# Layer 0 attention: the causal mask of the row maxima moves from TensorE's mask matmuls into VectorE's add-and-minimum instructions

## The reference

```python
Wdkv = x @ latent_w + latent_b
q = jnp.einsum('btc,hcl->bhtl', x, Wd_w) + Wd_b[None, :, None, :]
scores = jnp.einsum('bhtl,bsl->bhts', q, Wdkv) / jnp.asarray(np.sqrt(d_head), dtype=x.dtype)
causal = jnp.tril(jnp.ones((t, t), dtype=bool))
scores = jnp.where(causal[None, None, :, :], scores, -jnp.inf)
attn = jax.nn.softmax(scores, axis=-1)
y = jnp.einsum('bhts,bsl->bhtl', attn, Wdkv)
z = jnp.transpose(y, (0, 2, 1, 3)).reshape(b, t, h * Wdkv.shape[-1])
return z @ out_w + out_b
```

## Time and profile before

| | |
|---|---|
| median of 3 runs | 1755.58 us (1755.29 to 1759.24) |
| profiled execution, first to last instruction | 1746.9 us; its time outside that is not listed, and the median is 8.7 us over the span |
| PE busy | 1511.2 us (87%) |
| DVE busy | 1119.7 us (64%) |
| ACT busy | 997.0 us (57%) |
| POOL busy | 933.4 us (53%) |
| mean granted TensorE clock | 0.956 of full speed |
| mask matmuls L1843, first to last start | 45.2 to 791.5 us |
| one step | about 22.4 us (218 instructions of L962 in 610 us, eight to a step) |

### The profile page before, as it was taken

The page is one execution under the profiler, slowest core; times in us unless marked ns, Lnnn a source line. Parts: engine busy times, 40 slices in busy tenths (PEclk is TensorE's granted clock), DMA queues, the critical chain, the costliest instruction groups (busy, mean ns, idle before and its releaser), DMA issues. The chain is left out here.

```text
span 1746.9 us, 44836 instructions
## 1 busy us (share of the span) xinstructions
PE 1511.2 (87%) x14050; PEld 1109.0 (63%) x14051; DVE 1119.7 (64%) x2639; ACT 997.0 (57%) x2526; POOL 933.4 (53%) x1639
## 2 busy tenths in 40 slices
PE   4798999999999999998999488888888888885773
PEld 4655555555555555555998377777777777764662
DVE  3365555555555555553555399999899988985661
ACT  3343555555555555554332588888888888862441
POOL 6233555555555555554443666666666666632663
PEclk9998999999999999999999699999999999995875
DMA  7412222222222221223332021121211212116444
GB/s 197 133 29 57 55 55 55 55 55 55 56 56 56 56 56 56 56 59 75 68 70 60 22 49 45 41 44 43 46 43 41 44 44 45 42 31 123 89 90 113
DMA packets 240879, 107.53 MB, mean 62 GB/s; under 512 B 145465, under 2 KB 229242, under 8 KB 240762
## 3 DMA queue, kind: packets, MB, share of 16 engines
q1 hardware_dynamic: 230586, 93.23, 22.4%
q0 software_dynamic: 10240, 13.64, 3.7%
HBM read 61.92 MB, written 40.16 MB: 58 GB/s over the span
## 5 line engine op out<-in xcount | busy, mean ns | idle before, releaser
L670 POOL TENSOR_SCALAR_AFFINE_SELECT probs<-probs 128x512 f32<-128x512 f32 x256 | 183.5, 740 | 160.0 <-ACT probs L1515 160.0
L962 DVE TENSOR_REDUCE mneg<-bankS 128x2 f32<-128x256 f32 x256 | 107.2, 419 | 221.5 <-PE bankS L1848 220.9
L1515 ACT ACTIVATE probs<-bankT 128x1024 f32<-128x1024 f32 x128 | 131.0, 1023 | 185.2 <-PE bankT L1861 185.2
L963 DVE TENSOR_REDUCE mneg<-bankS 128x2 f32<-128x512 f32 x256 | 174.3, 681 | 0.0
L1510 ACT ACTIVATE qT<-bankA,bd 128x256 f32<-128x256 f32 x256 | 107.5, 473 | 95.0 <-PE bankA L1830 95.0
L1830 PE MATMUL bankA<-xnT,wd 128*128 128x256 f32 x512 | 149.7, 416 | 0.0
L663 POOL CAST qb<-qT 128x256 bf16<-128x256 f32 x256 | 97.1, 398 | 96.5 <-ACT qT L1510 96.3
L1858 PE MATMUL bankT<-qT,kT 37*128 37x512 f32 x512 | 136.9, 611 | 7.5 <-DMA qT<-mT 5.4
L1319 DVE STREAM_TRANSPOSE pt<-pe 128x768 f32<-128x768 f32 x128 | 124.4, 972 | 25.3 <-ACT pe L1600 25.1
L1875 PE MATMUL bankB<-probs,vaug 128*64 128x512 f32 x512 | 139.0, 621 | 1.1 <-ACT yT L1522 1.0
L1522 ACT COPY yT<-bankB 128x512 f32<-128x512 f32 x128 | 75.0, 586 | 82.1 <-PE bankB L1879 82.1
(11 more groups left out here) (316 smaller groups left out, 4315.6 us busy)
## 6 DMA issues: line engine op xcount, KB each, us to landing
rzb<-reciprocals SPq DMA_DIRECT2D x128, 128.0 KB
yT<-yT SPq DMA_DIRECT2D x64, 128.0 KB
xtab<-tab SPq DMA_DIRECT2D x32, 192.0 KB, 2.0
xs_sorted<-zeros SPq DMA_DIRECT2D x1, 4608.0 KB, 18.5
qT<-xs_sorted SPq DMA_DIRECT2D x144, 32.0 KB, 1.7
ys_sorted<-qT SPq DMA_DIRECT2D x36, 128.0 KB, 1.9
value_rows<-vrow SPq DMA_DIRECT2D x32, 128.0 KB, 1.8
vx<-value_rows SPq DMA_DIRECT2D x256, 16.0 KB, 1.8
```

The costliest lines, as they stand in the source:

```text
L670: pool.affine_select(out=blocks, in_=blocks, compare_op=ALU.is_ge, fill=0.0, base=0, pattern=[[0, 4], [1, P]], channel_multiplier=-1).then ...
L962: dve.tensor_reduce(mneg[:, n.half, :, j, 0], bankS[:, :, 0:128], AX.X, ALU.max, negate=True)
L963: dve.tensor_reduce(mneg[:, n.half, :, j, 1], bankS[:, :, 128:384], AX.X, ALU.max, negate=True).then_inc(S["red_done"], 1)
L1515: act.activation(pT[:, g % 2].rearrange("p e j t -> p e (j t)"), bankT[:, 0:2, :], ACT.Exp, scale=SCALE0).then_inc(S["exp_done"], 1)
```

## The change

The four mask matmuls of each `smax` go, with the constants `rowsel` and `rowneg` and the twelve GpSimd selections that make them. A constant `causal` of 128 x 256 float32 takes their place: 128 columns of zero, then the 128 x 128 mask with -1e30 above the diagonal. `red` now adds it to the scores while it takes the maximum: `tensor_tensor_reduce` computes (scores + mask) * -1 element by element, writes that to a scratch tile `masked`, and gives the minimum of a row, which is the negated maximum. One instruction does one row range of one head, so there are four instead of two. A `passed(dve)` stands ahead of them.

```diff
-            for e in range(2):
-                r = HALVES[e]
-                pool.affine_select(out=rowsel[r, 0, :], in_=rowsel[r, 0, :], compare_op=ALU.not_equal, fill=1.0, base=0,
-                                   pattern=[[-1, P]], channel_multiplier=1)
...
+            pool.affine_select(out=causal[:, P:2 * P], in_=causal[:, P:2 * P], compare_op=ALU.is_ge, fill=NEG, base=0,
+                               pattern=[[-1, P]], channel_multiplier=1)
...
             def red(n, j):
                 dve.wait_ge(S["s_ps"], n.b * PAIRS + (j + 1))
-                dve.tensor_reduce(mneg[:, n.half, :, j, 0], bankS[:, :, 0:128], AX.X, ALU.max, negate=True)
-                dve.tensor_reduce(mneg[:, n.half, :, j, 1], bankS[:, :, 128:384], AX.X, ALU.max,
-                                  negate=True).then_inc(S["red_done"], 1)
+                passed(dve)
+                for e in range(2):
+                    dve.tensor_tensor_reduce(masked[:, e, 0:P], bankS[:, e, 0:P], causal[:, P:2 * P], -1.0, -NEG, ALU.add, ALU.min,
+                                             mneg[:, n.half, e, j, 0:1])
+                for e in range(2):
+                    ins = dve.tensor_tensor_reduce(masked[:, e, P:3 * P], bankS[:, e, P:3 * P], causal[:, :], -1.0, -NEG, ALU.add, ALU.min,
+                                                   mneg[:, n.half, e, j, 1:2])
+                ins.then_inc(S["red_done"], 1)
...
-                for k in range(2):
-                    for e in range(2):
-                        blocks = bankS[:, e, 0:384].rearrange("p (i h c) -> p i h c", h=2, c=LP)[:, 0:3:2, k]
-                        pe.matmul(blocks, rowsel[HALVES[e], k, :], rowneg[HALVES[e], k, :].unsqueeze(1).to_broadcast([LP, 2, LP]),
-                                  start=(k == 0), stop=False, skip_group_check=True)
                 for e in range(2):
-                    pe.matmul(bankS[:, e, 0:128], qb[ROWS[e], j, 0:P], kb[ROWS[e], 0:P], start=False, stop=True, skip_group_check=True)
+                    pe.matmul(bankS[:, e, 0:P], qb[ROWS[e], j, 0:P], kb[ROWS[e], 0:P], start=True, stop=True, skip_group_check=True)
```

More of the change, by code:

```diff
@@ L155, in program @@
         ys_d = nc.dram_tensor("ys_sorted", [TILES * P, C], F32).ap()
-        rowsel = sb("rowsel", [P, 2, P], BF16)
-        rowneg = sb("rowneg", [P, 2, LP], BF16)
+        causal = sb("causal", [P, 2 * P])
+        masked = sb("masked", [P, 2, 3 * P], BF16)
         wd = sb("wd", [P, PAIRS, 2, LP])
@@ L558, in _ @@
             pool.memset(identb[:, :], 0.0)
[L559 to L562, removed]
+            pool.memset(causal[:, :], 0.0).then_inc(S["cst"], 1)
             pool.wait_ge(S["cst"], 3)
@@ L567, in _ @@
                                    pattern=[[-1, P]], channel_multiplier=1)
-            for e in range(2):
-                r = HALVES[e]
-                pool.affine_select(out=rowsel[r, 0, :], in_=rowsel[r, 0, :], compare_op=ALU.not_equal, fill=1.0, base=0,
-                                   pattern=[[-1, P]], channel_multiplier=1)
[L572 to L583, removed]
+            pool.affine_select(out=causal[:, P:2 * P], in_=causal[:, P:2 * P], compare_op=ALU.is_ge, fill=NEG, base=0,
+                               pattern=[[-1, P]], channel_multiplier=1)
             pool.affine_select(out=strict[:, :], in_=strict[:, :], compare_op=ALU.is_gt, fill=0.0, base=0,
                                pattern=[[1, P]], channel_multiplier=-1).then_inc(S["consts"], 1)
-            made = 7
+            made = 3
             def chain(ins):
@@ L1839, in smax @@
                     pe.wait_ge(S["red_done"], n.b * PAIRS + j)
-                for k in range(2):
-                    for e in range(2):
-                        blocks = bankS[:, e, 0:384].rearrange("p (i h c) -> p i h c", h=2, c=LP)[:, 0:3:2, k]
-                        pe.matmul(blocks, rowsel[HALVES[e], k, :], rowneg[HALVES[e], k, :].unsqueeze(1).to_broadcast([LP, 2, LP]),
-                                  start=(k == 0), stop=False, skip_group_check=True)
                 for e in range(2):
-                    pe.matmul(bankS[:, e, 0:128], qb[ROWS[e], j, 0:P], kb[ROWS[e], 0:P], start=False, stop=True, skip_group_check=True)
+                    pe.matmul(bankS[:, e, 0:P], qb[ROWS[e], j, 0:P], kb[ROWS[e], 0:P], start=True, stop=True, skip_group_check=True)
                 for e in range(2):
-                    ins = pe.matmul(bankS[:, e, 128:384], qb[ROWS[e], j, P:T], kb[ROWS[e], :], start=False, stop=True, skip_group_check=True)
+                    ins = pe.matmul(bankS[:, e, P:3 * P], qb[ROWS[e], j, P:T], kb[ROWS[e], :], start=True, stop=True, skip_group_check=True)
                 ins.then_inc(S["s_ps"], 1)
```

## The result

The changed kernel takes 1778.95 us (median of 4 runs, 1773.95 to 1782.39), the kernel before on the same chip 1756.11 (4 runs, 1755.29 to 1759.24): a ratio of 1.0124, 95% interval 1.0101 to 1.0147.

A forecast was written before the change was run, and what follows sets the result against it. Waits for VectorE's `red` were taken to hold PE in four links per step. Terms summed to +1.64 us a step, +46 for 28 steps, +3 for the first three: 1755.6 + 49 = 1805 us, range 1785 to 1845.

The forecast's parts named there:

- R: Time from first start to last end of a `red` on VectorE; forecast to grow from 1.02 to 1.47 us.
- links 0-1, 3-4, 5-6: Stretches from one `smax` to the next where PE waits for `red`; each forecast from 1.67 to 2.09 us, +0.42.
- link 1-2, with the reciprocal: From `smax` 1 to 2, also delayed by a reciprocal waiting for a DMA; forecast +0.42, less 0.2 us.
- links 2-3, 4-5: From `smax` 2 to 3 and 4 to 5, where PE's own work sets the pace; forecast to gain 0.13 us each.
- `smax` 6 to `kv` and on to the next 0: `red` 6, `normalise` and `red` 7 in a row on DVE; forecast from 4.02 to 4.44 us until `kv`, +0.42.
- The bound: In four links per step PE is held briefly by waits for `red`, hidden by its overlapping records.
- I take 0.07: Price in us of each accumulator read in `red`; four make 0.28, and the last one's tail adds 0.08.
- the cover: PE's work that hid `red` 7 ahead of `kv`, with 0.16 us to spare; forecast to be used up.
- The marker: `passed` between the wait and `red`'s first instruction; costs between 0 and 0.24 us, taken as 0.10.
- The reciprocal's delay: The reciprocal's DMA wait delays `red` 1; with a later `smax` 1 it was to go, -0.2 us a step.
- The rival in which the reads ride along: Accumulator reads in `red` add no spacing, `red` takes 1.20 us, not slower: 1756 us; chance 0.08.
- The rival of no overlap: Each `red` instruction waits until the one before leaves the engine; +5.24 us a step, 1908 us; chance 0.20.

The follow-up runs named there:

- e1: Fused masking instructions and the marker added to the kernel before, with the mask matmuls kept on PE; 1790.6 us, ratio 1.0190.
- e2: The kernel before without mask matmuls and without fused instructions, so the scores go unmasked into the old reductions; 1737.9 us, ratio 0.9889.
- e9: The kernel before with only the marker `passed(dve)` added ahead of the two old reductions; 1762.8 us, ratio 1.0041.
- e12: The changed kernel with VectorE's reciprocal moved behind the reduction of pair 1; 1764.2 us, ratio 1.0042 against the kernel before.
- e5: The kernel before with the first two `av` matmuls of a group drawn ahead of `smax` 2 and 4; 1758.5 us, ratio 1.0021.

## Why the prediction was wrong

| term of a step, us | forecast | measured |
|---|---|---|
| R | 1.02 to 1.47 | 1.02 to 1.19 |
| scores of a `smax` to the first main | 0.37 to 0.47 | 0.37 to 0.53 |
| links 0-1, 3-4, 5-6 | +0.42 each | +0.22 to 0.23 each |
| link 1-2, with the reciprocal | +0.42 - 0.2 | +0.24 |
| links 2-3, 4-5 | -0.13 each | -0.13 each |
| `smax` 6 to `kv` and on to the next 0 | +0.42 | -0.06 |
| sum | +1.64 | +0.60 |
| 28 steps | +46 | +17 |
| first three steps | +3 | +0.2 (fourth step's first scores: 174.8 to 175.0) |
| clock at half in 5 steps | not in the sum | +8 |

The last scores of layer 0 start 24.4 us later (791.6 to 816.0); the table has 25. What lies behind them, which no kernel of the study changes, takes 955 to 965 us in the 14 traces, and the fourth step's first scores lie at 170.3 to 177.3 us: so much do single executions differ, and +0.2 is no measurement of that term.

*The bound was right.* In the step shown `smax` 1, 2, 4 and 6 start 0.15 to 0.16 us behind the last read, with the waits written beside them, and e1 and e2 show it by halves. PE's falling busy time was a gain of 18 us alone (e2), which the 35 us of VectorE's half (e1) outweigh.

*The step that failed* is "I take 0.07, since a read has one element per partition and comes behind an instruction of the same kind of stream". The mains were right (0.215 and 0.34 forecast, 0.21 and 0.345 measured), and the four reads cost nothing between them; only the last one's 0.08 stands at the end. That is 0.28 us of R, in four links and twice in 6 to `kv`. The price was taken from tiny instructions back to back; those read an input, while the row of the read has no input (`mneg<-`). The prediction's own lower bound was right, but its range stopped at 1785, which no row supported; nor does a free marker give it, since 0.10 in four links and once ahead of `kv` is 0.5 us a step, 14 us, and so 1791.

*`smax` 6 to `kv`* followed from R: 0.53 from scores to `red` 6, 1.11 until `normalise` (420.71 to 421.82), 1.03 until `red` 7 (422.85), 1.18 until its last read ends (424.03), 0.14 to `kv` at 424.17, in all 3.99. The form of the sum held; with R at 1.19 the cover was not used up.

*The marker* costs 0.11 (e9), as taken. From the scores to the first main it is 0.53, though, and not 0.47: 0.05 beyond the marker was not foreseen, and no run shows where it comes from.

*The reciprocal's delay did not go.* The term of -0.2 let `smax` 1 come later and left the reciprocal's DMA where it was: "their DMAs are no later against PE than before, beyond 0.15 us". The trace shows otherwise. On SyncE that DMA (L372) stands behind the four DMAs of the maxima (L364), which wait for `red` 7. First after, then before:

```profile
424.52 2.24 SPq L364 DMA_DIRECT2D qT<-mT  x4
...
429.98 0.57 SPq L372 DMA_DIRECT2D dq<-remainders  x1
```

```profile
419.36 0.57 SPq L372 DMA_DIRECT2D dq<-remainders  x1
```

It is issued 5.95 us behind the end of `red` 7 after (424.03) and 5.96 before (413.40), and it lands about 8 us behind that end in every trace that shows its landing (medians 7.99 to 8.12). A longer `red` 7 thus comes back as a later reciprocal in the next step. `red` 7 ends 0.33 us later against the next step's scores, since `kv` had room (it stood 0.31 behind `red` 7 and now stands 0.14 behind it) and the masks ahead of the scores are gone. So the reciprocal starts 2.39 us behind the scores of `smax` 0 instead of 2.04 (medians), and the scores of `smax` 1 moved by 0.22 only. In e1 the reciprocal starts at 2.20 and `smax` 1 comes at 1.98; there link 1 to 2 is 1.99, like its equals of 1.98, and the delay is gone, as the prediction argued for its larger R. e12 shows that in after this order costs 0.23 us a step, and that without it no half clock came.

*The rival in which the reads ride along* had R right, 1.20, and its time of 1756 wrong: each link grew by 0.22, not 0.15 (0.07 x 4 x 28 = 8 us), the reciprocal's 0.2 did not go (6 us), and the half clock (8 us) makes 1778. The clock was named beforehand, at a chance of 0.04 for "something else" and without a size. The rival of no overlap, and with it the rule of the Trainium skill, "VectorE: DVE Perf Modes", section "The DRAIN you can't avoid", by which the next op waits for an empty pipe (save one that is not held, as the section adds), fell: 286 ns mains (mean of 420) start 0.21 apart. Its 5.64 kept two overlaps of 0.09 that it denies; without them it would have been 5.82, and 5 us more in time.

## What to carry to other kernels

Moving work from a busy engine to one with room pays only in the links where the first one sets the pace: list the waits from step to step, and price both forms link by link, since the best kernel here uses each form where it is free. An operation that no row shows belongs into the range with its whole bound, from nothing on. And look for a DMA's wait that stands in an in-order list ahead of work that someone waits for: moving that one instruction gave 9 us without the change and 15 with it. Follow the DMA back, too, to what it is queued behind, since that can be what the change makes longer.

## What the runs showed of the hardware that was not expected

- The read of an accumulator (82 ns, mean of 420) starts together with the next main instruction and adds nothing.
- A semaphore marker between a wait and the first instruction costs 0.11 us (e9).
- TensorE's clock fell to 0.50 for 3.4 us in the midst of a steady loop, four times behind two waits in a row (0.48 us, then 0.38 to 0.57), at 1.64 us a time; other steps with such waits stayed at 1.00, and so did all with a second wait of 0.18 to 0.25 (e12).
- The DMA for the reciprocals landed about 8 us behind the end of `red` 7 in each kernel, since SyncE issues it behind the DMAs of the maxima (7.99 to 8.12).
- Splitting a group of `av` matmuls around an `smax` costs PE 0.16 us (e5).
